# One chain of eight blocks on one core: context keys and values projected in the first stage, a norm in two halves, and the reciprocals of channel attention behind its maxima

## The reference

```python
x = x + wkv(w, u, layernorm(x), ctx)                 # stage 0, a recurrence over tokens
x = x + top1_attention(layernorm(x), W_gate, W_qkv)  # stage 1, self attention, 16 heads of 16
x = x + int8_cross_attention(layernorm(x), ctx, ...) # stage 2
x = x + fp8_product(layernorm(x), input2)            # stage 3
x = x + channel_attention(layernorm(x), ctx, ctx)    # stage 4, 8 channels to a head, 256 x 256 scores
x = x + ternary_ffn(layernorm(x), w_gate_up, w_proj) # stage 5
x = x + batch_attention(layernorm(x), ctx, ctx)      # stage 6
x = x + experts(layernorm(x), gate_w, w1, w2, w3)    # stage 7
```

```python
q = qdq(x) @ qdq(wq).T + bq          # x is the layernorm of the residual
kv = cond @ wkv.T + bkv              # cond is the context: keys and values do not depend on x
attn = softmax(q_h @ k_h.T / 4)      # per batch entry, 16 heads, 64 keys
out = qdq(attn @ v) @ qdq(wp).T + bp
```

## Time and profile before

| | us |
|---|---|
| median of three runs | 908.04 |
| the profiled execution | 906.22 |
| its span, first to last instruction | 904.5 |
| granted TensorE clock, mean over the span | 0.889 of full |
| busy: PE, DVE, ACT, POOL | 650.3, 522.1, 288.7, 239.6 |
| chain that ended last: PE, DVE, issue, POOL | 49%, 23%, 6%, 5% |

### The profile page before, as it was taken

How to read it: one execution, slowest core, us unless ns; L and a number is a source line. 1 busy time by engine, 2 the same in 40 slices (tenths; PEclk the granted TensorE clock), 3 DMA queues, 4 the chain that set the end, 5 groups by cost and what they waited for, 6 DMA issues and landing times.

```text
span 904.5 us, 10915 instructions
## 1 busy us (share of the span) xinstructions
PE 650.3 (72%) x3659; PEld 416.4 (46%) x3660; DVE 522.1 (58%) x1108; ACT 288.7 (32%) x530; POOL 239.6 (26%) x228
## 2 busy tenths in 40 slices
PE   1025888878863149777755999565299999999991
PEld 1013354654552115544434667444156666666661
DVE  7986686586957898989865543464522212221223
ACT  5601233234334505654554333142012111211110
POOL 3210441137800073065292003200111121112100
PEclk9999998699957558998897999895599999999996
DMA  6000002000204463542120000796100000000004
GB/s 233 0 0 0 1 10 62 1 1 1 59 1 106 125 152 81 138 118 67 61 72 12 1 1 1 318 413 261 54 18 24 24 29 29 23 23 29 23 12 152
DMA packets 34142, 61.85 MB, mean 68 GB/s; under 512 B 6232, under 2 KB 29784, under 8 KB 31768
## 3 DMA queue, kind: packets, MB, share of 16 engines
q1 hardware_dynamic: 22592, 45.78, 15.9%
q10 hardware_dynamic: 9296, 9.44, 3.2%
q0 software_dynamic: 2208, 6.03, 2.1%
HBM read 47.35 MB, written 13.50 MB: 67 GB/s over the span
## 4 chain that ended last, share of the span: by engine, by line
PE 49%; DVE 23%; issue 6%; POOL 5%; ACT 3%; DMA 1%; SPq 0%; ACTq 0%; POOLq 0%; DVEq 0%
PE bank L1691 15%; PE bank L1712 7%; DVE region L1126 5%; PE bank L1331 5%; PE bank L1350 3%; PE bank L558 3%; PE bank L1702 2%; PE bank L532 2%; DVE XN L356 2%; PE bank L1029 2%; PE bank L544 1%; ACT region L1390 1%; PE bank L990 1%; PE bank L1829 1%; POOL rstd L370 1%
## 5 line engine op out<-in xcount | busy, mean ns | idle before, releaser
L1691 PE MATMUL bank<-region,wide 128*128 x368 | 143.7, 544 | 0.3 <-issue 0.3
L1595 DVE TENSOR_TENSOR wide<-wide,bank 128x448 f32<-128x448 f32 x46 | 28.6, 621 | 125.0 <-ACT wide L1638 78.6
L1691 PEld LDWEIGHTS bank<-region,wide 128*128 128x128 f32 x368 | 68.8, 192 | 61.4 <-issue 61.2
L1126 DVE TENSOR_REDUCE region<-bank 128x2 f32<-128x512 f32 x128 | 80.2, 682 | 9.9 <-PE bank L990 9.2
L1052 ACT ACTIVATE region<-bank 128x1024 f32<-128x1024 f32 x64 | 65.4, 1026 | 47.5 <-PE bank L1013 43.9
L990 PE MATMUL bank<-region 128*128 128x256 bf16 x256 | 54.1, 314 | 30.5 <-DMA region<-norm_parts 21.3
L1712 PE MATMUL bank<-region,XN 128*128 x322 | 73.4, 379 | 1.3 <-DVE wide L1608 1.3
L1499 POOL DMA_INDIRECT choice_results<-wide,to_row x23 | 22.8, 990 | 181.6 <-DVE wide L1608 181.6
L1712 PEld LDWEIGHTS bank<-region,XN 128*128 128x128 f32 x322 | 59.5, 190 | 9.4 <-issue 2.3
L1638 ACT ACTIVATE wide<-bank 128x448 f32<-128x448 f32 x46 | 25.0, 544 | 111.9 <-PE bank L1691 111.9
L370 POOL TENSOR_TENSOR rstd<-vareps,half_neg 128x8 f32<-128x8 f32 (+1 forms) x10 | 14.9, 1489 | 163.5 <-DVE vareps L350 131.3
(11 more groups left out here) (298 smaller groups left out, 1247.7 us busy)
## 6 DMA issues: line engine op xcount, KB each, us to landing
region<-in_L_ffn_experts_dram SPq DMA_DIRECT2D x8, 2688.0 KB, 19.2
region<-ctx_parts SPq DMA_DIRECT2D x24, 192.0 KB
region<-norm_parts SPq DMA_DIRECT2D x24, 192.0 KB
channel_values<-wide ACTq DMA_DIRECT2D x8, 512.0 KB, 5.0
ctx_parts<-region SPq DMA_DIRECT2D x40, 64.0 KB, 2.1
wide<-in_L_ffn_w_gate_up_dram ACTq DMA_DIRECT2D x4, 512.0 KB, 4.3
wide<-channel_values SPq DMA_DIRECT2D x16, 128.0 KB, 2.5
norm_parts<-region SPq DMA_DIRECT2D x24, 64.0 KB, 4.6
```

The lines of the kernel that those rows point to most:

```text
L1126: e.tensor_reduce(nmax[i % 2][:, at_:at_ + KC], score_bank("scores", n).rearrange("p (c n) -> p c n", c=KC), AX.X, ALU.max, negate=True).t ...
L1595: e.tensor_tensor(HB8[par][:, cols], silu8[:, cols], bank[hf][:, 512:512 + I8 // 2], ALU.mult)\
L1691: last = e.matmul(bank[hf][:, 512 * gu:512 * gu + hw], xbT[par][:, P * c:P * c + P], region[:, bass.ds(off + (2 * gu + c) * I8 + hw * hf, ...
```

## The change

Context keys and values are projected in stage 0, PE's part right behind the first turning of XN, ACT's behind its exponentials, and lie in `wide` until stage 2. The norm and rounding of stage 2 are done in two halves of four tiles: the first in the drain of self attention, the second in the first steps of cross attention; their turnings and the query projections follow by halves. POOL begins its keys of stage 2 once the first half is rounded. In stage 4 the maxima are turned before they are split: PE transposes the float32 maxima, DVE splits them out of PSUM, one step later, and ACT's copy is gone. The reciprocals stand behind the loop of maxima, four sets of buffers take the loaded values, and the ternary work comes in four steps on four successive pairs at other places.

The diff, cut to its core:

```diff
@@ buffers
-        KT = carve(KC, N)
-        V = carve(NT, D)
+        KT = wide[:, 0:KC * N].rearrange("p (a b) -> p a b", a=KC)
+        V = wide[:, KC * N:KC * N + NT * D].rearrange("p (a b) -> p a b", a=NT)
-        nrest = [carve(TU * KC) for j in range(2)]
-        nparts = [carve(3, TU * KC, dt=BF16) for j in range(2)]
-        nmaxT = [carve(P, dt=BF16) for j in range(2)]
+        nmaxT = [carve(3, P, dt=BF16) for j in range(2)]
-        NUM5 = [wide[:, 4 * N + D * j:4 * N + D * j + D] for j in range(2)]
+        NUM5 = [wide[:, at + D * j:at + D * j + D] for at in (4 * N, 0) for j in range(2)]
+        SETS = len(NUM5)
@@ pool_attention, s == 1
+                pool_norm(e, 2, 0, 4)
+                e.wait_ge(s_att["k_ready"], 2 * KC)
+                e.wait_ge(s_att["v_copied"], NT)
+                e.wait_ge(s_att["norm_quantised"], 4)
                 for i in range(NT):
                     kbd(i)
                     e.tensor_tensor(V[:, i, :], V[:, i, :], bvrow, ALU.add).then_inc(s_att["v_ready"], 1)
                     e.wait_ge(s_att["v_ready"], i + 1)
+                    if i == 1:
+                        pool_norm(e, 2, 4, NT)
                     pool_context_part(e, ch, 1, i - 1)
@@ pe_attention
+            def quantised_T(hf, first):
+                e.wait_ge(s_att["norm_quantised"], 4 * hf + 4)
+                turn_half(XN, hf, first)
+            def queries(hf, first):
+                e.wait_ge(s_turned, TURN["att1"] + KC * (hf + 1))
+                project_half(wqT, 0, XT, hf, first, s_att["q_in_psum"])
@@ the loop over t
                 for f, lag in ((scores, 1 + L), (key_T, 1), (values, 3 + L), (probs_T, 2 + L)):
+                    if s == 1 and t == 3 and f is values:
+                        queries(1, 4)
                     if 0 <= t - lag < NT and not (s == 1 and f is key_T):
                         f(t - lag)
+                if s == 0 and t == NT + 2:
+                    e.wait_ge(s_att["kv_selected"], NT)
+                    quantised_T(0, 6)
+                if s == 0 and t == NT + 3:
+                    queries(0, 6)
+                if s == 1 and t == 2:
+                    e.wait_ge(s_att["out_normalised"], NT)
+                    quantised_T(1, 4)
@@ vec_attention: quantise_norm(lo, hi) is the norm and rounding of before, on tiles lo to hi
+                if s == 0 and t == NT:
+                    e.wait_ge(x_done, NT + 4)
+                    norm_variance(e, ch, 2, 0, 4, first=3)
+                if s == 0 and t == NT + 1:
+                    quantise_norm(0, 4)
+                if s == 0 and t == NT + 2:
+                    vec_f8_weights(e, ch)
+                if s == 0 and t == NT + 3:
+                    e.wait_ge(x_done, 2 * NT)
+                    norm_variance(e, ch, 2, 4, NT, first=NT - 1)
+                if s == 1 and t == 1:
+                    quantise_norm(4, NT)
@@ sp_channel
-                if i >= 2:
+                if 2 <= i < SETS + 2:
                     values_in(e, i - 2)
...
+            for i in range(SETS, NT):
+                values_in(e, i)
@@ values_in
-            if i >= 2:
-                e.wait_ge(x_done, 4 * NT + i - 1)
+            if i == 2:
+                e.wait_ge(s_tern["weights_cast"], 5)
+            if i >= SETS:
+                e.wait_ge(x_done, 4 * NT + i - SETS + 1)
@@ pe_channel, maxima_T
-                e.wait_ge(s_chan["maxima_split"], i + 1)
+                e.wait_ge(s_chan["maxima_ready"], 2 * w + 2)
                 bank_free(e, "maxima", i)
-                e.transpose(turned_maxima(i), nparts[i % 2].rearrange("p a b -> p (a b)"),
-                            identb[:, :]).then_inc(s_chan["maxima_turned"], 1)
+                e.transpose(turned_maxima(i), nmax[i % 2], ident[:, :]).then_inc(s_chan["maxima_turned"], 1)
@@ pool_channel_tiles
+            WEIGHTS = {0: (0, 1, 2, 3), 2: (4,), 4: (5,)}
-            e.wait_ge(s_chan["maxima_split"], 1)
             for i in range(NT):
-                if i < TW // TCH:
-                    pool_ternary_weights(e, ch, i)
+                for c in WEIGHTS.get(i, ()):
+                    pool_ternary_weights(e, ch, c)
                 add_values(e, ch, i)
@@ vec_channel
+            WEIGHTS = {17: 2, 35: 3}
+            def maxima_parts(w):
+                if w % TP5 != TP5 - 1:
+                    return
+                i = w // TP5
+                e.wait_ge(s_chan["maxima_turned"], i + 1)
+                if i >= 2:
+                    e.wait_ge(s_chan[f"maxima_in{i % 2}"], 48 * (i // 2))
+                split3(e, ch, turned_maxima(i), turned_maxima(i), [nmaxT[i % 2][0:TU * KC, j, :] for j in range(3)])\
+                    .then_inc(s_chan["maxima_split"], 1)
+            def weights(w):
+                for first, c in WEIGHTS.items():
+                    if 0 <= w - first < 4:
+                        vec_ternary_step(e, ch, c, w - first)
-            pair_steps([(weights_early, 0), (maxima, 0), (invert, BEHIND + 14), (weights_late, BEHIND + 14)])
+            pair_steps([(maxima, 0), (maxima_parts, 1), (weights, 0)])
+            for i in range(NT):
+                invert(i)
+                if i == 1:
+                    for c in (4, 5):
+                        for step in range(4):
+                            vec_ternary_step(e, ch, c, step)
@@ tensor block
+            def context_keys_values():
+                e.wait_ge(s_loaded["ctxT"], 16)
+                e.wait_ge(s_loaded["wkv"], 80)
+                for hf in range(2):
+                    project_half(wkvT, 0, CT, hf, KC * hf, s_att["k_in_psum"])
+                for i in range(NT):
+                    e.wait_ge(s_att["k_ready"], i // 2 + 1)
...
             token_to_channel(XN, 4, s_xn, 0)
+            context_keys_values()
             for g, (_, srcs) in enumerate(blocks):
+                e.wait_ge(s_att["v_copied"], 2 * g + 2)
                 if g == 0:
                     e.wait_ge(s_dq, 4)
@@ scalar block, behind the four units' exponentials
+            leave(KT, 0, s_att["k_in_psum"], s_att["k_ready"], bkcol)
+            for j in range(NT // 2):
+                e.wait_ge(s_att["v_in_psum"], 2 * j + 2)
+                e.activation(V[:, 2 * j:2 * j + 2, :].rearrange("p t d -> p (t d)"), ps(j), ACT.Copy)\
+                    .then_inc(s_att["v_copied"], 2)
```

More of the change, by code:

```diff
@@ L357, in norm_tiles, with norm_variance @@
                                 rstd[:, i:i + 1], ALU.subtract, ALU.mult).then_inc(s_xn, 1)
-        def norm_variance(e, ch, s, lo, hi):
-            for i in range(lo, hi):
+        def norm_variance(e, ch, s, lo, hi, first=None):
+            for i in range(lo if first is None else first, hi):
                 last = e.bn_stats(stats[:, 6 * i:6 * i + 6], X[:, D * i:D * i + D])
@@ L448, in pool_attention, with pe_attention @@
                         pool_blank_keys(e, ch, i - 2)
-        def pe_attention(e, s, token_to_channel):
+        def pe_attention(e, s, token_to_channel, turn_half, project_half):
             e.wait_ge(s_wt, 2)
             e.wait_ge(s_loaded["wqkv"], 32)
[L454 to L463, removed]
             if s == 0:
                 token_to_channel(XN, 0, s_xn, NT)
[L467 to L485, removed]
+            def quantised_T(hf, first):
[4 more added lines that the diff above has]
+                project_half(wqT, 0, XT, hf, first, s_att["q_in_psum"])
             def key_value(i):
@@ L581, in pe_attention, with act_attention, quantised_T, queries @@
                     last.then_inc(s_att["projected"], 1)
[L583 to L592 removed]
+        def act_attention(e, ch, s, leave, turned, leave_half):
+            if s == 0:
+                turned(XT, 0, "att0")
+            def quantised_T(hf, first):
+                leave_half(XT, hf, first, s_turn, s_turned, base=TURN["att1"])
+            def queries(hf, first):
+                leave_half(QT, hf, first, s_att["q_in_psum"], s_att["q_ready"], bqcol, base=4)
             def gate_sum(i):
@@ L646, in act_attention @@
             for t in range(NT + 5):
+                if s == 1 and t == 3:
+                    queries(1, 4)
                 for f, lag in ((key_T, 1), (value_blocks, 2 + L), (probs, 1 + L), (probs_T, 2 + L)):
@@ L1874, in leave, with leave_half @@
             def leave(dst, first, full, done, bias=None, base=0):
-                for g in range(2 * KC):
-                    c, hf = g % KC, g // KC
-                    e.wait_ge(full, base + g + 1)
+                for hf in range(2):
+                    leave_half(dst, hf, first + KC * hf, full, done, bias, base)
+            def leave_half(dst, hf, first, full, done, bias=None, base=0):
+                for c in range(KC):
+                    e.wait_ge(full, base + KC * hf + c + 1)
                     d = dst[:, c, 512 * hf:512 * hf + 512]
                     if bias is None:
-                        e.activation(d, ps(first + g), ACT.Copy).then_inc(done, 1)
```

(5 more changed lines are left out.)

162 lines of the change are left out of this document (76 added, 86 removed).

## The result

| | before | after |
|---|---|---|
| median, us (4 runs each, same chip) | 907.87 | 886.44 |
| lowest to highest | 906.81 to 908.68 | 886.02 to 887.04 |
| profiled execution | 906.22 | 886.02 |
| its span | 904.5 | 884.2 |
| busy: PE, DVE, ACT, POOL | 650.3, 522.1, 288.7, 239.6 | 647.3, 521.8, 285.7, 239.9 |

The account below looks back on a forecast made before the run. No engine bounds the whole span; each stage has its own limit. 906.2 - 4.3 (seam) - 11.1 (channel stage with drain) = 890.8 profiled, median 892.0; own range 887 to 897, whole range 881 to 902.

Parts of the forecast that it names:

- the second rival: Seam: DVE takes the port before POOL, gaining 12.5 us in place of 4.3, so 884; chance 0.20.
- First stage, nothing: First stage: the added key and value projections cost nothing, hidden in PE's idle time; values copied by 47.
- The seam, 4.3: Between the two attentions: norm and queries by halves, tile 0 normalised at 213.9 in place of 218.20, 4.3 us gained.
- more from the seam: Seam: DVE takes the port first, second half takes 6.4 us, 12.5 gained in place of 4.3; chance 0.20.
- The channel maxima, 16.0: Channel stage: splits from PSUM no longer wait for POOL; PE issues its last values 16.0 us sooner.
- The 12.8 and the 3: Channel stage: 12.8 us lost by three splits meeting POOL, about 3 by PE's half clock behind them; both go.
- The price of 0.6: Channel stage: 0.6 us taken off the 21.3 us excess; a split was put at 1.5 us against 1.1.
- such small things, 0.8: Channel stage: 0.8 us of the 21.3 us excess, beside slow splits, half clock and ternary blocks.
- less from the channel: Channel stage: PSUM splits or the ternary steps meet POOL, 16.0 becomes 3.2, so 902; chance 0.20.
- The drain, 5.3 lost less 0.4 for the statistics: End of channel stage: POOL's longer work sets the end, 5.3 us less gained than PE's; statistics give 0.4.
- Maxima in time: Channel stage: the maxima's transfers take 7.4 us against PE's five steps of 8.3, a slack of 0.9.
- that rival: Channel stage: maxima come late at every tile, up to 4.7 us at seven boundaries, 912 to 925; chance 0.08.

Follow-up runs that it names:

- the two profiles with a seam of 114.5 us: Attention part alone put into the kernel before, 901.57 us; and the changed kernel with DVE's ternary block 4 in the channel loop, 885.16 us.
- the kernel in which POOL holds back: Changed kernel, but POOL waits for the second half of the quantised norm before its key blocks of tile 2 of cross attention; 883.56 us.
- the run with them: Changed kernel, but DVE first copies the turned maxima out of PSUM and splits them from SBUF; 911.08 us.
- the experiment with block 4 moved: Changed kernel, but DVE's steps for ternary block 4 lie in the channel loop and POOL's part before its first add; 885.16 us.

## Why the prediction was right

Every part went the way forecast, and the three main mechanisms (POOL stretching the second half, the split from PSUM, POOL's queue in the drain) are shown by experiment. The sizes of two terms were too small by 4.9 us together: the sum gave 890.8 for the profiled execution, which took 886.02. The median of 886.44 lies in the whole range, 881 to 902, but 0.6 us below the 887 to 897 that the forecast gave for its own mechanism, and nearer to the 884 of the second rival than to 892. The time alone would not tell the two apart; the rows do.

**First stage, nothing.** Right: values copied by 46.9 (forecast 47), L1885 at 48.74.

**The seam, 4.3; measured 6.1.** Up to the end of the second half the steps held: the first half ended at 169.9 (forecast 169.9), the last value products began at 173.3 (173.3), the scores at 183.4 (182.6), the second half ended at 201.5 (201.5). That the last two agree so well is in part luck: the half began at 187.8, 0.7 late, and took 13.8 us, not 14.3. The excess that POOL adds to it was 7.7 us (4.6 in L355, 2.7 in L673, 0.4 in a small one) against 7.9; the single instructions took from 0.3 to 2.3 us, not 2 each. Mis-sized was what follows. The second two query blocks ran wholly at full clock, 3.70 us against the 4.7 taken, which was a value between the two levels. The first two had granted clock 0.50 until 181.0 and 1.00 behind it, and took 5.98 against 5.1. The scores took 2.62 against 2.8. Tile 0 was normalised at 212.96 (213.9), 5.2 us sooner than before. Another 0.9 us came behind it, in work that the change does not touch: tiles 4 and 5 were 6.59 us apart before and 5.97 after, and the projection at the end took 9.01 in place of 9.23; the forecast had no term for it. Both belong to this execution more than to the change. In the two profiles with a seam of 114.5 us the second query blocks took 3.83 and 3.84, the scores 3.68, one spacing is 6.6 as before, and the seam's gain is 4.7 us, close to the 4.3.

The rival "more from the seam" did not happen: DVE did not get the port first. Its price can be read from the kernel in which POOL holds back: there tile 0 is normalised 46.68 us behind the mark of tile 5, against 56.81 before, 10.1 gained of the 12.5 told.

**The channel maxima, 16.0; measured 17.8 over the same 23 intervals.** The excess over 3.31 us an interval fell from 21.3 to 3.5 us, not 5.3. The 12.8 and the 3 went; that splits from SBUF would have cost such sums again, the run with them shows. The price of 0.6 for longer, later splits did not come up: outside the ternary steps all intervals but one are 3.31 or 3.32 us. The two ternary blocks cost PE 1.7 and 1.4 us between the marks, not 2.35 each; that the four steps spread them over DVE's slack would explain it, but no run shows it. The last 0.4 is in an interval without ternary work (3.67 us), where before had one of 3.68; the forecast counted such small things, 0.8, as gained without saying why. The rival "less from the channel" is out by the same rows.

**The drain, 5.3 lost less 0.4 for the statistics; measured 3.9.** PE's last value products moved from 469.71 to 445.52, 24.2 us of which 6.1 were there before the stage: 18.1. The stage as a whole gained 14.2 (forecast 11.1), so 3.9 went in the drain, 4.9 by the forecast. POOL's last add ended 35.5 us behind the last split (forecast 36.6; before 32.7), and the statistics 0.5 us sooner behind it (0.4). The cause was as told, POOL's queue with blocks 4 and 5 ahead of the late tiles; the experiment with block 4 moved shows it.

**Maxima in time.** The slack was taken as 0.9 us and is about 2; the chance of that rival was rather too high for it. Which of its terms was too long is not shown.

## What to carry to other kernels

Where a short chain on DVE falls under POOL's work, look at what it reads before asking where it stands: five instructions of 0.2 to 0.3 us from SBUF became 10 us in one place, and reading from PSUM cost at most 0.07 each. Where one engine's queue is the seam between two stages, the order on it is worth as much as its length: taking unrelated work and a shift away from in front of the critical half gained 3.9 us on the kernel in which POOL holds back (109.26 to 105.36), and cutting that work to fit the idle time where it went another 2.7. Together that is as much as the change itself had gained there. Of a moved wait, ask what stands behind it next: here POOL's queue, then a transfer.

## What was not expected

Two profiles of the same changed kernel have tile 5 of self attention at 161.76 and 161.81 us, but across the profiles of kernels that are alike up to there it lies between 161.2 and 166.9, and single runs of one kernel spread from 882.0 to 893.6 us. In a good stretch (granted clock 1.00 from 115 to 124 us of the kernel after) the tiles are 9.3 us apart; from 134 to 146.4 the clock is 0.75 and the gap 12.1 us. The profile of the kernel with block 4 in the loop has three such gaps in a row, with 0.77, 0.80 and 0.77. A difference of 2 or 3 us in a median cannot be told from that in four runs; the intervals between marks can tell it in stage 4, and in the seam only where the clock is compared too.

With POOL held back, the scores of tile 2 began 4.0 us sooner than after, but the clock rose to 1.00 only 1.5 us sooner (at 203.5 in place of 205.0), so they ran wholly at half clock.
